# A four-layer network in one launch: the expert pass of the last layer and two vector passes of the Mamba layer re-split over VectorE, GpSimd, ScalarE and TensorE, with a new order table

## The reference, cut to what matters

```python
dt = jax.nn.softplus(dt @ Wdt.T + bdt)
h = dA * h + dt_t[:, :, None] * B_t[:, None, :] * u_t[:, :, None]
y = jnp.einsum('bds,bs->bd', h, C_t)
...
y = jnp.swapaxes(ys, 0, 1) + u * Dp
y = y * jax.nn.silu(z)
return y @ Wo.T
```

```python
w = jax.nn.silu(jnp.einsum('btd,bthkd->bthk', hidden_states, de) * jax.nn.softmax(scores, axis=-1))
experts_states = jnp.einsum('bthk,bthkd->btd', w, ue)
```

## Time and profile before

| | us |
|---|---|
| three runs: median (lowest to highest) | 1951.8 (1943.66 to 1962.64) |
| the profiled execution, its own time | 1944.52 |
| span of its trace | 1942.6 |

### The profile page before, as it was taken

One profiled execution on the slowest core, in us unless ns is written; L12 is line 12 of the kernel. 1 busy time (PEld: TensorE's weight loads), 2 busy tenths in 40 slices (PEclk: granted clock), 3 DMA queues, 4 the chain that ended last, 5 costly groups with the idle time before them and its releaser, 6 DMA issues. The chain is left out here.

```text
span 1942.6 us, 27894 instructions
## 1 busy us (share of the span) xinstructions
PE 1489.4 (77%) x9225; PEld 1050.3 (54%) x9225; DVE 1613.5 (83%) x2548; ACT 1290.1 (66%) x2656; POOL 1215.0 (63%) x1667
## 2 busy tenths in 40 slices
PE   4777665666888888576778999778888886789976
PEld 1343333334566666444345776656666665668755
DVE  5389899898989899999899798999988999962266
ACT  3476656655867678776687767788776776753453
POOL 2248576677666678876676575786786777640043
PEclk9677777766989999898798899989898998889997
DMA  5022223433533344211343444422445442112300
GB/s 184 1 66 66 69 64 77 93 74 87 141 99 103 109 131 107 66 25 42 85 112 94 115 120 126 110 80 54 122 123 131 126 126 66 54 40 77 114 17 6
DMA packets 84591, 170.15 MB, mean 88 GB/s; under 512 B 9440, under 2 KB 14944, under 8 KB 84064
## 3 DMA queue, kind: packets, MB, share of 16 engines
q1 hardware_dynamic: 84448, 168.37, 32.2%
...
## 5 line engine op out<-in xcount | busy, mean ns | idle before, releaser
L1037 POOL TENSOR_TENSOR m<-m 128x256 f32<-128x256 f32 x1024 | 912.2, 925 | 179.3 <-DVE m L1026 143.4
L1026 DVE TENSOR_TENSOR_SCAN m<-m,dtuB 128x1024 f32<-128x1024 f32 x256 | 584.0, 2281 | 17.5 <-ACT m L1004 2.2
L1004 ACT ACTIVATE m<-m,Aneg 128x255 f32<-128x255 f32 x1024 | 427.7, 497 | 47.6 <-DMA m<-m 36.1
L1018 DVE TENSOR_TENSOR dtuB<-m 128x1024 f32<-128x1024 f32 x256 | 345.5, 1349 | 18.6 <-DMA m<-m 11.5
L1434 PE MATMUL ps<-o 128*128 128x256 f32 x512 | 156.9, 418 | 31.4 <-DVE X L1378 16.6
L1401 ACT ACTIVATE o<-ps,w_mo 128x256 f32<-128x256 f32 x256 | 113.8, 471 | 98.3 <-PE ps L1434 97.2
L1050 PE MATMUL ps<-m,w_const 128*32 128x256 f32 x2048 | 158.5, 432 | 20.7 <-POOL m L1037 20.5
L360 POOL TENSOR_TENSOR o<-o,mhalf 128x2 f32<-128x2 f32 x64 | 21.9, 343 | 213.3 <-DVE o L354 213.1
L1152 PE MATMUL ps<-o 128*128 128x256 f32 x512 | 131.2, 405 | 14.7 <-ACT o L1121 11.0
L943 PE MATMUL ps<-m,wc 128*128 128x256 f32 x512 | 134.3, 421 | 8.1 <-ACT m L381 8.0
L1442 PE MATMUL ps<-o 128*128 128x128 f32 x1024 | 135.2, 287 | 4.3 <-ACT o L1401 3.5
...
## 6 DMA issues: line engine op xcount, KB each, us to landing
m<-m SPq DMA_DIRECT2D x256, 256.0 KB, 4.9
...
o<-in_mox SPq DMA_DIRECT2D x128, 256.0 KB, 3.2
...
```

Source lines behind the costliest of these rows:

```text
L1004: op = e.activation(dA[at % NA][:, j, 1:CH], R[q][:, h * CH + 1:h * CH + CH], ACT.Exp, scale=Aneg[:, l, 4 * g + j:4 * g + j + 1])
L1018: e.tensor_tensor(dtuB[:, :, :], bc(R[q][:, (2 + h) * CH:(3 + h) * CH].unsqueeze(1), 4, CH), Br[k % 2], ALU.mult).then_inc(S.dve, n.tick(f ...
L1026: e.tensor_tensor_scan(flat(G[at % NG]), flat(dA[at % NA]), flat(dtuB[:, :, :]), 0.0, ALU.mult, ALU.add).then_inc(S.dve, n.tick(f"s{g}"))
L1037: op = e.tensor_tensor(part, part, Cr[k % 2][:, j:j + 1, :], ALU.mult)
```

## The change

Three edits, and a new order table.

1. **Lookup.** A tile `md` (the first half of `hid`) takes md = (E >= s8) * D in one pass on DVE, E from SBUF and D from PSUM. POOL then forms w = E * md (both in SBUF), and ACT's silu gets `scale=rinv`. As there is one `md`, DVE's pass of a head waits for POOL's pass of the head before.
2. **Mamba, u*D.** Setup forms diag(D) for each layer on POOL, over the first half of the input weights that nothing reads any more. PE adds diag(D) @ u to `S.y` by two 128x128x256 matmuls in front of the sums over the states; the two DVE passes are gone.
3. **Mamba, dt*u.** The 128x512 pass moves from DVE to POOL; SP's DMA of dt*u now waits for POOL.

```diff
                 if k >= 2:
                     c, l = UNITS[k - 2]
                     e.wait_ge(S.pe, S.at(k - 2, "pe", "y7"))
-                    for h in range(2):
-                        y = S.y[:, h * CH:h * CH + CH]
-                        e.scalar_tensor_tensor(y, v.u[:, h, :], m("dp", l)[:, h:h + 1], y, ALU.mult, ALU.add).then_inc(
-                            F.dve, n.tick(f"ud{h}"))
-                    e.wait_ge(F.dve, n.dve("ud1"))
                     e.tensor_tensor(v.dtu, halves_of(S.y), v.z, ALU.mult).then_inc(F.dve, n.tick("y"))
...
-                e.wait_ge(F.dve, n.dve("dt"))
-                e.tensor_tensor(v.dtu, v.dt, v.u, ALU.mult).then_inc(F.dve, n.tick("dtu"))
                 yield
...
                 norm_pool(e, n, F, v)
+                yield
+                e.wait_ge(F.dve, n.dve("dt"))
+                e.tensor_tensor(v.dtu, v.dt, v.u, ALU.mult).then_inc(F.pool, n.tick("dtu"))
                 yield
...
+                l = UNITS[k][1]
+                e.wait_ge(U.pool, U.at(0, "pool", f"dp{l}"))
+                e.wait_ge(F.act, F.at(k, "act", "u1"))
+                for h in range(2):
+                    e.matmul(S.y[:, h * CH:h * CH + CH], m("win", l)[:, h * 128:h * 128 + 128], chains[k % 2].u[:, h, :],
+                             start=h == 0, stop=False, skip_group_check=True)
+                yield
...
-                    for p in range(2):
-                        for h in (2 * p, 2 * p + 1):
-                            Eh = v.Em[h % 2]
-                            e.wait_ge(T.pool, n.pool(f"E{i}{h}"))
-                            e.scalar_tensor_tensor(Eh, Eh, v.s8[:, h, 7:8], Eh, ALU.is_ge, ALU.mult).then_inc(T.dve, n.tick(f"E{i}{h}"))
-                            yield
-                        for h in (2 * p, 2 * p + 1):
-                            Eh = v.Em[h % 2]
-                            e.wait_ge(T.pe, n.pe(f"D{i}"))
-                            e.wait_ge(T.dve, n.dve(f"E{i}{h}"))
-                            e.scalar_tensor_tensor(Eh, o[:, :], v.rinv[:, h:h + 1], Eh, ALU.mult, ALU.mult).then_inc(
-                                T.dve, n.tick(f"w{i}{h}"))
-                            yield
+                    e.wait_ge(T.pe, n.pe(f"D{i}"))
+                    for h in range(4):
+                        e.wait_ge(T.pool, n.pool(f"E{i}{h}"))
+                        if i or h:
+                            e.wait_ge(T.pool, n.pool(f"w{i}{h - 1}" if h else f"w{i - 1}3"))
+                        e.scalar_tensor_tensor(v.md, v.Em[h % 2], v.s8[:, h, 7:8], o[:, :], ALU.is_ge, ALU.mult).then_inc(
+                            T.dve, n.tick(f"w{i}{h}"))
+                        yield
...
+                        for h in (2 * p, 2 * p + 1):
+                            e.wait_ge(T.dve, n.dve(f"w{i}{h}"))
+                            e.tensor_tensor(v.Em[h % 2], v.Em[h % 2], v.md, ALU.mult).then_inc(T.pool, n.tick(f"w{i}{h}"))
+                            yield
...
-                            e.wait_ge(T.dve, n.dve(f"w{i}{h}"))
+                            e.wait_ge(T.pool, n.pool(f"w{i}{h}"))
                             table(e, "silu")
-                            e.activation(Eh, Eh, ACT.Silu).then_inc(T.act, n.tick(f"w{i}{h}"))
+                            e.activation(Eh, Eh, ACT.Silu, scale=v.rinv[:, h:h + 1]).then_inc(T.act, n.tick(f"w{i}{h}"))
```

All five strings of the order table are new; of POOL's, the first line before and now:

```diff
-        "ua2baub2u4afafba2fb2sfs4bs5fs6afs6as2bfa2s10fs6b2afs4bs6fs7fsfs6baf2s6bs2asfsas8fasbs3bs3fs8fbs4as2asa2sfs7a6fs6"
+        "ua3b3u5aufafabu3fabfbsfs4bfs5fs6af2s6afs2bafas6fs5fs5babf2bs5fs6fs5f2sfs7bfaf2s5fbs3afs4asfs5fasbs3fs3bsfs5fs2bf"
```

More of the change, by code:

```diff
@@ new lines @@
+        "a9ua4ub2a4babababab2aba3b6abab2ab4a3bab2afafb2fbaf2asab2ab2a5b2a3fa2fa2f3sa2b3ab2ab2sb2fbab3sbf2saf3ab2sbf2ab3ab"
+        "f2asf2bsa6bsfa3fa4bfbas2abf3a7b2asbfa4sbf2safaf2sb2fasf2baf2bfabsb9sbfb5sbfsfbf3sfa3b3af2s2f3safa2b2a2bafafab2fa"
+        "fbfa2bs2ababasbfa3bfafafbsa2fbafsa3ba5b2abasafba2b2fabafasfbfsfa2bab2a4ba2b2sba2fa2ba2b2sa2fbfb2f2sfb3a2ba2ba2sb"
+        "a2bafa5fba2bfa3bafa2fbasbfasb3ab7ab3sfb2ab2sa2bf2ba2bfabsf2b2ab2sfb6a2bfb3fsb2afb2afa2sfbaba5bsbfba2b2fbasba3fa3"
+        "fbfbafsa3b2aba2ba2ba6sbabfb3asab2f4asb2fb9sb2abfsbabab2abfbfa2fbfa2safbaba3sa2bfbf2a2bf3as2b4a3bab2safsa2bfbfafa3"
@@ new lines @@
+        "b5ababa4b4ab5a2bababa",
+    "dve":
+        "a8u4bub7a11bafafb5a5ba2b4fb2sfs2fs4bsbs3bsbsb3fs8fsf2s7as3a2f2a2f2s2as8aba3sas2fa2s3ab2a3faba2sfbfbs10bs2bsb2fs2"
+        "bs5fs2f2s3as6ab2af2a2bf2bab3sbsbs9afs10fs2f2s9a3f2af2s3fsbs12bafab2fbsbf2safabsasab2sb2s6fb2s7a2bfsf2s2a3sbsabs2"
+        "abs2asafsasasas2as2as2fsaf2sa2s2babs6afbsb2asbsbsfbsasf2bs2bs2bs2bs2asbsbfsabs2fsbabf2s2as3bsas4ba2fs2abas2bas2f"
+        "a2f2bs6a2sasbs5afa2bfa2f2sasbs3asabsas4b2s2a5baba2fbas2b2a3s4asafsf2safa3sa3b6sb3s4b3sfs3b4sb4abs2afbafb2fa2fab2"
+        "s4bsbsb3absbs6fa4fsf2s3a2s7asasabsasfb2sb2sbsfsf2s6bs3b2sbabfasbsbs3a3sfaf2b2s2absabasas2as2afs2as2as2as2fa2f2s5"
+        "b2as3as2bafb2sabsbsbabs2bs2bfasbsbsf2bsabs3b2as3bsafbs2a2sbfsafafbasa2sbs4bsfs2a3bsa6bs2abs2a2b2sfsbf2a3fasabsa3"
+        "bas2basbafas3a2s2ba2s2asbab4sfb2f2s2fbs2b2sbasas5b4sba3bab2afbas2ab2asbas2ab2sfsf2sabs2abs3bas3bfa2s3as3fs2f2as4"
+        "as2b2s5f2bab2f2s3abs2bs2bs2bs2bs2bs2fbsab2sfsf2sbsbsbsasbs2bs4afs2bs2as2bfsf2sbs4bs4bfs2a2sbsasabsfaf2sa2b2s5bs2"
+        "a6ba2fabs2baba2s4a6ba2fab2sab2a2fsbsa2b3s2asa2basb2s4b5sbsb2sba2b3safabafaba3baba2b2a6b2abab4ab5ab3ab2abab3ab2a2"
+        "b2a2ba3b5a3b2a6b3abab2ab3abab2a4ba2b5ab4ab2a2ba",
@@ L252 @@
+        "s2fs2afa2sas5a4fa5s2abfbfsa4ba5sabsas2fs3b3fbfb5sbs2as2ab4sb5fbs2bsfs5afs4fs3bs3f2bs7fsfsbs5fs3fs5fsa2s2afabs4ba4"
+        "faba4bas3a10b3absb5sbs4b9abs2ba2b3a4b4a10b10a4b4ab2ab2aba2ba",
 }
@@ L505, in pool @@
                     yield
-                e.wait_ge(U.pool, n.pool(f"wc{NL - 1}"))
+                e.wait_ge(loaded["const"], 16)
+                for l in range(NL):
+                    e.wait_ge(U.pool, n.pool(f"wc{l}"))
+                    e.tensor_tensor(m("win", l)[:, 0:CH].rearrange("p (h c) -> p h c", h=2), bc(ident.unsqueeze(1), 2, 128),
+                                    bc(m("dp", l).unsqueeze(2), 2, 128), ALU.mult).then_inc(U.pool, n.tick(f"dp{l}"))
+                    yield
                 for i in range(NA):
@@ L972, in sp @@
                 for q in range(4):
-                    for w, name in enumerate(("dt", "dtu")):
-                        e.wait_ge(F.dve, F.at(k, "dve", name))
+                    for w in range(2):
+                        e.wait_ge(*((F.pool, F.at(k, "pool", "dtu")) if w else (F.dve, F.at(k, "dve", "dt"))))
                         if k and w == 0:
@@ L1050, in pe @@
                             op = e.matmul(S.y[32 * q:32 * q + 32, h * CH:h * CH + CH], red, G[(8 * k + g) % NG][:, j, :],
-                                          start=h == 0 and j == 0, stop=j == 3, skip_group_check=True)
+                                          start=False, stop=j == 3, skip_group_check=True)
                             if j == 3:
@@ L1612, in pool @@
                     e.wait_ge(T.act, n.act(f"ss{i}"))
-                    for h in range(4):
-                        if h == 2:
+                    for p in range(2):
+                        if p:
                             e.wait_ge(T.dve, n.dve(f"ri{i}"))
```

75 lines of the change are left out of this document (31 added, 44 removed).

## The result

| | before | after |
|---|---|---|
| median of the comparison's runs | 1949.7 us (1943.7 to 1962.6) | 1899.3 us (1890.2 to 1901.2) |
| ratio, 95% interval | | 0.9721 [0.9671, 0.9771] |
| profiled execution: time, span | 1944.5, 1942.6 us | 1890.2, 1888.3 us |

The change makes the kernel 2.8% faster. The ratio is that of the means of the runs (1897.0 and 1951.4 us); the medians give 2.6%. In the later comparisons the kernel before had medians of 1941 to 1945 us, and against those 1899.3 us would be 2.2 to 2.4%, so the size is known to about half a per cent. The forecast was 1905 in a range of 1852 to 1955.

A forecast was written before the change was run, and what follows sets the result against it. The prediction took VectorE, busy 90.5% of the middle, as nearest to bounding it, with the tail set by chains of single steps. Middle -46 and tail +6 gave -40 from 1944.5, so 1904.5 us, range 1852 to 1955.

The forecast's parts named there:

- VectorE's lost work: Whole kernel: VectorE loses masks, u*D and dt*u, -99.1 us busy in the middle and 17 in the tail, to about 1497.
- The new GpSimd pass: Middle: GpSimd gains 80 passes of 128x512 at 1.4 us each, +112 us (86 to 148).
- The masked pass: Lookup: VectorE's new pass, one SBUF and one PSUM operand, takes 738 ns like the old product, without spread.
- TensorE and ScalarE: Middle: 27 us of u*D matmuls and 17 us of table loads are hidden; the silu's scale costs nothing new.
- Where the lookups lie: Three middle stretches, 479 us: GpSimd becomes the fuller engine, so the gain is 26 us, not 53.
- The rest of the middle: The other 1133 us: VectorE loses 46.2 us, of which rather under half counts, -20 us.
- What waits behind dt*u: Middle: C passes on GpSimd and SP's DMAs wait behind dt*u; extra hop covered by the other chain's scan, 0.
- Tail: After the middle: 0.7 us more for each of 8 pairs of heads, +6 us (0 to +20).
- The whole gain: Rival, whole kernel: VectorE's idle time stays at 153 us, middle -99, tail +6, about 1852 us; chance 0.2.
- Nothing to be seen: Rival, middle: the chain of front, scan and norm across engines sets its length; gain under 19 us, about 1940; chance 0.2.
- The slower one: Rival, middle: the shared path of VectorE's and GpSimd's SBUF passes bounds; middle +55, about 2005 us; chance 0.12.

The follow-up runs named there:

- all three undone: Changed kernel's new order table kept, with the lookup, u*D and dt*u edits all taken out: 1943.3 us, 1.0008 of the kernel before.
- the doubled product: Changed kernel with GpSimd's 128x512 product in the lookup done twice in place: 1976.2 us, 1.0164 of the kernel before.

## Why the prediction was right, point by point

**VectorE's lost work.** Forecast 1497 us in all, 116 less; measured 1514.6, 99 less, of them 85 in the middle where 99.1 were forecast. The edited lines are not the reason: all 64 masks, u*D and dt*u are gone, and the masked pass has 47.6 us in the place of the old product's 45.3. Line by line, VectorE's other lines add 8 us, none of them more than 3. The other 7 us are no work: busy time is counted once where the records of two lines overlap, and there is 7 us less such overlap now.

**The new GpSimd pass.** The line through the 128x256 and 128x1024 rows gave 1267 ns undisturbed; the median is 1268. The 1.4 us taken for contention was too much: the means are 1299 and 1333. GpSimd's busy time is 1316.9, not 1350: 9 us for that reason, 12 because the C passes got a little shorter (925 to 913 ns), and the rest is spread over its small passes.

**The masked pass.** 0.73 to 0.75 us without spread was forecast from its PSUM operand; it takes 717 to 750. The old mask, with two SBUF operands, took 719 to 1539. The Trainium skill's "SBUF — State Buffer", "Who interferes with whom", says that an instruction of VectorE with at most one SBUF input, outside the two-port modes that the page names, does not contend with GpSimd. The trace agrees.

**TensorE and ScalarE.** Both put at nothing. u*D is 40.9 us of matmuls and not 27: 64 matmuls show as 128 records of 450 ns in the mean, where the step took 64 at 421. It is hidden all the same: without u*D's matmuls the time is the same (0.9767 against 0.9721, the middle 1554.3 against 1554.5). The main group of table loads rose from 77 to 84, 9 us, with ScalarE at 75% in the middle. "The scale costs nothing new" was wrong: the silu with `scale=rinv`, one value per partition, takes 704 to 737 ns, without it 612 to 632. In the changed kernel's order it has a median of 722 with the scale and 629 without (all three undone), 93 ns more and 6 us for the 64; whether any of it shows in the time was not tested.

**Where the lookups lie.** The step said that GpSimd becomes the fuller engine, as full as VectorE had been, and takes back half of VectorE's gain. The size was right: unit by unit, at the same order, 56 us less on VectorE gave 27 us, where 26 of 53 were forecast. The direction held too: less VectorE work is worth next to nothing there now, and less GpSimd work is worth 13 us in these units and 24 in all. The reason given fits only in part. GpSimd is at 82 to 84%, not over 90%, no fuller than VectorE, so a full GpSimd is not what was seen; its load, or the way from the product to the silu and the transposes, would both do, and no run separates them. The lookup's edit as a whole is worth 8 to 18 us by the reading.

**The rest of the middle.** "Rather under half" of 46 us, -20, was sized too low. At the same order the other 23 units became 28 us shorter. They lost only 33 us of VectorE's busy time, not 46, but gave back most of it, not under half. The row from 411 us showed both engines full and was weighed too heavily. Against the kernel before, the new order itself takes 3 us of middle back (1605.6 to 1608.7), so the middle lost 51 us where 46 was forecast. That these two lie so near is partly luck: the share was too low, the work taken away was put too high, and the order's 3 us were not in the sum.

**What waits behind dt*u.** Priced at 0, since "the extra hop is covered by the other chain's scan". In the changed kernel that holds: 10.30 us from `dt` to the first product against 10.40. But the cover is given by the order: the other chain's scan is there in before's order as well, and the same step costs 39 us of middle. The prediction named the places (the C passes behind it, SP's queue) and left out the chain itself, dt*u's lateness for its own scan.

**Tail.** Forecast +6, measured +0.7 between two executions with the same clock of 0.96 in the tail's first 40 us. One pair of heads in the tail, as in the earlier trace rows:

```profile
1822.83 2.04 POOL L1632 TENSOR_TENSOR o<-o 128x512 f32<-128x512 f32 x2
...
1823.97 0.75 DVE L1597 SCALAR_TENSOR_TENSOR o<-o,ps 128x512 f32<-128x512 f32 x1 [0.44 <-POOL o L1632]
...
1824.83 1.26 POOL L1637 TENSOR_TENSOR o<-o 128x512 f32<-128x512 f32 x1
...
1826.19 0.75 DVE L1597 SCALAR_TENSOR_TENSOR o<-o,ps 128x512 f32<-128x512 f32 x1 [1.41 <-POOL o L1637]
...
1827.02 1.27 POOL L1637 TENSOR_TENSOR o<-o 128x512 f32<-128x512 f32 x1 [0.93 <-DVE o L1597]
...
1827.60 1.45 ACT L1675 ACTIVATE o<-o 128x512 f32<-128x512 f32 x2
```

From E's start to the second product's end it takes 5.46 us where 5.6 was forecast and 4.94 stood before. The end that counts, though, is the silu's. The first product is ready at 1826.09, so the table load is not held up and the silus start 4.77 us after E and not 5.50 as in the earlier trace rows; longer as they are, they end 6.22 us after E and not 6.65. The lower bound named in that step was the right value. The upper bound, 20 us for 16 more products in line, is what the doubled product costs in the tail.

**The rivals.** The whole gain (1852) did not come; the changed kernel comes no nearer to it than 1890. "Nothing to be seen" is out by the interval. The slower one asked for scan products 0.3 us longer; they went from 1349 ns in the mean to 1353 with 102 us more on GpSimd (from 1331 at the same order), so it is out by a factor of ten and more. A way to be slower did exist, the late dt*u, and no rival named it.
